# Routed feed-forward: expert results scaled by the token's share and added by indirect DMA onto the output, in place of stored pair rows that are read back

## The reference, cut to what matters

```python
logits = jnp.einsum('bsd,de->bse', input_emb, Wr) + br          # input_emb = layernorm(x); 8 experts
route_w = jax.nn.softmax(logits, axis=-1)
_, topk_idx = jax.lax.top_k(route_w, TOP_K)                     # TOP_K = 2
mask = jax.nn.one_hot(topk_idx, E, dtype=route_w.dtype).sum(-2)
routed = route_w * mask
routed = routed / routed.sum(axis=-1, keepdims=True)            # the two shares of a token
h = jax.nn.relu(jnp.einsum('bsd,edh->ebsh', input_emb, W1) + b1[:, None, None, :])
expert_out = jnp.einsum('ebsh,ehd->ebsd', h, W2) + b2[:, None, None, :]
return jnp.einsum('bse,ebsd->bsd', routed, expert_out)          # and x = x + this is the output
```

## Time and profile before

| What | Value |
|---|---|
| Median of three runs | 2058.24 us (2058.22 to 2061.71) |
| The profiled execution: its own time, its span | 2056.44 us, 2054.1 us |
| Mean granted TensorE clock, share of full speed | 0.956 |
| Start of `routed_ffn` on PE | 1718.7 us |
| First hidden layer, tile 0 | 1770.1 us |
| Hidden layer of tile 2, and of tile 22 | 1790.7 us, 2012.5 us |
| Last matmul ends | about 2028.4 us |
| First and last addition onto X by DVE | 2037.2 us, 2049.9 us |

### The profile page before, as it was taken

The page is one execution under the profiler, slowest core; times in us unless marked ns, Lnnn a source line. Parts: engine busy times, 40 slices in busy tenths (PEclk is TensorE's granted clock), DMA queues, the critical chain, the costliest instruction groups (busy, mean ns, idle before and its releaser), DMA issues. The chain is left out here.

```text
span 2054.1 us, 40735 instructions
## 1 busy us (share of the span) xinstructions
PE 1817.9 (88%) x16084; PEld 1324.4 (64%) x16084; DVE 1519.5 (74%) x3172; ACT 1133.2 (55%) x1916; POOL 158.7 (8%) x129
## 2 busy tenths in 40 slices
PE   7959258997799999999999999988997897799994
PEld 6844155665466666666666666655674466688884
DVE  6987886667777777777777776787766777688886
ACT  3535754556366666666666665526542654467762
POOL 0001300000000000000000000000000100244431
PEclk9979689998999999999999999999999998799997
DMA  6120001003000000000000000010001001577775
GB/s 222 47 79 0 0 1 52 2 3 114 21 22 22 22 21 22 22 22 22 23 24 24 15 1 1 1 53 2 3 21 56 1 3 46 187 255 245 248 258 173
DMA packets 80365, 120.90 MB, mean 59 GB/s; under 512 B 9840, under 2 KB 62512, under 8 KB 80048
## 3 DMA queue, kind: packets, MB, share of 16 engines
q1 hardware_dynamic: 75760, 106.22, 15.6%
q0 software_dynamic: 4416, 12.06, 1.7%
HBM read 103.58 MB, written 14.68 MB: 58 GB/s over the span
## 5 line engine op out<-in xcount | busy, mean ns | idle before, releaser
L2586 PE MATMUL sl_ps_eo<-sl_w,sl_hT 128*128 128x256 f16 x3072 | 353.2, 273 | 0.8 <-DVE sl_hT L2829 0.7
L2563 PE MATMUL sl_ps_h<-sl_slot_inT,sl_w 128*128 128x512 f16 x1536 | 338.3, 379 | 0.5 <-ACT sl_h L2706 0.5
L2586 PEld LDWEIGHTS sl_ps_eo<-sl_w,sl_hT 128*128 128x128 f16 x3072 | 298.5, 98 | 35.8 <-DVE sl_hT L2829 1.3
L2706 ACT ACTIVATE sl_h<-sl_ps_h,sl_b1T 128x512 f32<-128x512 f32 x256 | 175.6, 687 | 170.3 <-PE sl_ps_h L2563 163.3
L2563 PEld LDWEIGHTS sl_ps_h<-sl_slot_inT,sl_w 128*128 128x128 f16 x1536 | 149.9, 98 | 176.3 <-ACT sl_h L2706 2.4
L2829 DVE TENSOR_TENSOR sl_hT<-sl_h,sl_hT 128x512 f16<-128x512 f32 x256 | 176.8, 692 | 102.2 <-ACT sl_hT L2709 97.9
L1149 DVE TENSOR_REDUCE at_neg_max<-at_ps 128x8 bf16<-128x1024 f32 x96 | 116.9, 1220 | 68.2 <-PE at_ps L831 68.2
L2125 PE MATMUL mo_ps_h<-mo_xgT,mo_w 128*128 128x256 f16 x1104 | 125.9, 275 | 3.5 <-issue 2.1
L2843 DVE SCALAR_TENSOR_TENSOR sl_result<-sl_ps_eo,sl_b 128x256 f32<-128x256 f32 x128 | 54.3, 424 | 97.8 <-PE sl_ps_eo L2586 93.5
L2136 PE MATMUL mo_ps_eo<-mo_w,mo_hT 128*128 128x256 f16 x1104 | 124.1, 273 | 0.0
L2125 PEld LDWEIGHTS mo_ps_h<-mo_xgT,mo_w 128*128 128x128 f16 x1104 | 108.1, 99 | 19.0 <-issue 5.8
(11 more groups left out here) (435 smaller groups left out, 3629.8 us busy)
## 6 DMA issues: line engine op xcount, KB each, us to landing
mo_w_raw<-in_L_ffn_W SPq DMA_DIRECT2D x46, 1024.0 KB, 8.7
sl_w_in<-in_L_ffn_w SPq DMA_DIRECT2D x16, 1024.0 KB, 5.4
at_ctxT<-ctx_pairs SPq DMA_DIRECT2D x9, 512.0 KB, 7.3
mo_w_raw<-pair_rows SPq DMA_DIRECT2D x4, 1024.0 KB, 9.0
mo_b<-in_L_ffn_b SPq DMA_DIRECT2D x23, 128.0 KB, 4.9
ac_attention_w<-L_attention_w SPq DMA_DIRECT2D x3, 768.0 KB, 12.4
w_pairs<-ac_w_pair SPq DMA_DIRECT2D x3, 768.0 KB, 3.2
ac_ctx_all<-in_ctx SPq DMA_DIRECT2D x4, 512.0 KB, 8.2
```

What stands on the lines that cost most here:

```text
L2563: last = pe.matmul(ps_h[:, j % 2], w1[:, e % 2, w, k, j * P:(j + 1) * P], slot_inT[:, q % 2, x, k].rearrange("p b s -> p (b s)"), start=(k ...
L2586: last = pe.matmul(ps_eo[:, b % 2, 0:D], hT[:, hp, j, b * P:(b + 1) * P], w2[:, e % 2, w, j], start=(j, a) == (0, 0), stop=(j, a) == (HJ - ...
L2706: act.activation(h[:, j % 2], ps_h[:, j % 2], ACT.Gelu, bias=b1T[:, q // G4, j:j + 1], scale=1.0 / W_SCALE).then_inc(h_ready, 1)
```

## The change

The scaling by the shares moves from the end of the phase into the tile loop, and the sum over a token's two experts moves from DVE to the DMA engines.

- SP writes X to the output at the phase's start (2 MB, and 256 KB more into spare rows behind it); the output tensor has 256 rows more, which the host cuts off.
- A row of `x_rows` grows from 1,024 to 1,032 bytes: behind the two halves stand the token's two shares, written by one DMA in pieces of 8 bytes (2,048 of them) once DVE has them. The gathers wait for it too, and bring the shares with the rows.
- POOL picks the right share of each slot with two small operations (`weigh`), which stand ahead of the tile's gather and scatter.
- ACT multiplies `y` by that share into `y_scaled` (`scaled`), two operations of 128 x 256 a tile, behind the copy of the next tile's rows.
- POOL's scatter adds onto the output (`compute_op=ALU.add`), and waits until the scatters of the tile before have landed, since two experts may add to the same token.
- SP's wait before the biases is now on `result_ready`, DVE's semaphore of `y`; DVE's `y` waits for ACT (`y_ready`) in place of the scatter.
- The read-back, DVE's 32 additions and the final stores are gone; SP only waits for the last scatters.
- DVE makes `to_i` behind `from_i`, and three small operations for the parity of a slot.

```diff
+            sp.dma_start(env.out[0:B * L].rearrange("(b l) d -> l b d", l=L), env.X[:]).then_inc(x_out, 16)
+            sp.dma_start(env.out[B * L:].rearrange("(b l) d -> l b d", l=L), env.X[:, 0:HALVES]).then_inc(x_out, 16)
...
+            sp.wait_ge(share_ready, 1)
+            with nc.allow_non_contiguous_dma("two shares a token"):
+                sp.dma_start(env.x_rows.rearrange("(b l) d -> l b d", l=L)[:, :, D:D + 2], shares[:]).then_inc(shares_out, 16)
             sp.wait_ge(expert_ready, 1)
...
                 if m >= WB:
-                    sp.wait_ge(y_ready, HALVES * (m - WB + 1))
+                    sp.wait_ge(result_ready, HALVES * (m - WB + 1))
...
-            pairs = env.pair_rows[0:2 * B * L].rearrange("(b l i) d -> l b i d", l=L, i=2)
-            for g in range(4):
-                sp.dma_start(yt[:, 4 * g:4 * g + 4], pairs[:, 4 * g:4 * g + 4]).then_inc(y_in[g], 16)
-            for g in range(8):
-                sp.wait_ge(x_done, 2 * (g + 1))
-                sp.dma_start(env.out[2 * g:2 * g + 2].rearrange("b l d -> l b d"), env.X[:, 2 * g:2 * g + 2]).then_inc(stored, 16)
...
+            def scaled(m, s):
+                act.wait_ge(result_ready, HALVES * m + s + 1)
+                act.wait_ge(weight_ready, m + 1)
+                enough(act, scattered[m % 2], 16 * HALVES * (m // 2))
+                act.activation(y_scaled[:, m % 2, s], y[:, m % 2, s], ACT.Copy, scale=weight[:, m % 2, s:s + 1]).then_inc(y_ready, 1)
...
+                if m >= 1:
+                    for s in range(HALVES):
+                        scaled(m - 1, s)
...
+            def weigh(m):
+
+                pool.wait_ge(gathered[m % XB], 16 * HALVES * (m // XB + 1))
+                pool.tensor_tensor(picked[:, m % 2], xg_rows[:, m % XB, :, D:D + 2], of_pair[:, HALVES * m:HALVES * (m + 1)],
+                                   ALU.mult).then_inc(picked_made, 1)
+                pool.wait_ge(picked_made, m + 1)
+                enough(pool, y_ready, HALVES * (m - 1))
+                pool.tensor_tensor(weight[:, m % 2], picked[:, m % 2, :, 0], picked[:, m % 2, :, 1], ALU.add).then_inc(weight_ready, 1)
+
             def scatter(m):
+                if m >= 1:
+                    pool.wait_ge(scattered[(m - 1) % 2], 16 * HALVES * ((m - 1) // 2 + 1))
                 for s in range(HALVES):
                     q = HALVES * m + s
                     pool.wait_ge(y_ready, q + 1)
-                    pool.indirect_dma_start(env.pair_rows, bass.IndirectOffsetOnAxis(ap=to_i[:, q:q + 1].bitcast(U32), axis=0),
-                                            y[:, m % 2, s], None).then_inc(scattered[m % 2], 16)
+                    pool.indirect_dma_start(env.out, bass.IndirectOffsetOnAxis(ap=to_i[:, q:q + 1].bitcast(U32), axis=0),
+                                            y_scaled[:, m % 2, s], None, compute_op=ALU.add).then_inc(scattered[m % 2], 16)
...
                 dve.wait_ge(eo_made, HALVES * m + s + 1)
-                enough(dve, scattered[m % 2], 16 * HALVES * (m // 2))
+                enough(dve, y_ready, HALVES * (m - 1))
```

More of the change, by code:

```diff
@@ L1955, in routed_ffn @@
         ratio = t.sb("ratio", [P, B, 1])
-        share = t.sb("share", [P, 2, B, 1])
+        shares = t.sb("shares", [P, B, 2])
         hit = t.sb("hit", [P, 2, B, E])
@@ L2015, in routed_ffn @@
         h_made, h_ready, h_high, h_split = (t.sem(n) for n in ("h_made", "h_ready", "h_high", "h_split"))
-        eo_made, y_ready = t.sem("eo_made"), t.sem("y_ready")
+        eo_made, result_ready, y_ready = t.sem("eo_made"), t.sem("result_ready"), t.sem("y_ready")
+        share_ready, shares_out = t.sem("share_ready"), t.sem("shares_out")
+        to_ready, of_pair_ready = t.sem("to_ready"), t.sem("of_pair_ready")
+        picked_made, weight_ready = t.sem("picked_made"), t.sem("weight_ready")
+        x_out = t.sem("x_out")
         scattered = [t.sem(f"scattered{i}") for i in range(2)]
-        y_in = [t.sem(f"y_in{i}") for i in range(4)]
-        first_added, x_done, stored = t.sem("first_added"), t.sem("x_done"), t.sem("stored")
         block = ctx.enter_context(nc.Block())
@@ L2197, in _ @@
                     tokens_out(m + 1)
+                if m >= 1:
+                    for s in range(HALVES):
+                        scaled(m - 1, s)
+            for s in range(HALVES):
+                scaled(NTILES - 1, s)
         @block.gpsimd
@@ L2258, in _ @@
             dve.wait_ge(ratio_ready, 1)
-            link(dve.tensor_scalar(share[:, 1], ratio[:], 1.0, None, ALU.add))
-            link(dve.reciprocal(share[:, 0], share[:, 1]))
-            link(dve.tensor_tensor(share[:, 1], share[:, 0], ratio[:], ALU.mult))
+            link(dve.tensor_scalar(shares[:, :, 1:2], ratio[:], 1.0, None, ALU.add))
+            link(dve.reciprocal(shares[:, :, 0:1], shares[:, :, 1:2]))
+            dve.tensor_tensor(shares[:, :, 1:2], shares[:, :, 0:1], ratio[:], ALU.mult).then_inc(share_ready, 1)
             dve.wait_ge(ranked, 1)
@@ L2297, in _ @@
             link(dve.scalar_tensor_tensor(spare[:], used[:], 1.0, spare_row[:], ALU.subtract, ALU.mult))
-            dve.tensor_tensor(to_i[:], pair[:], spare[:], ALU.subtract)
             dve.tensor_scalar(from_i[:], pair_i[:], 1, None, ALU.logical_shift_right).then_inc(table_ready, 1)
+            dve.tensor_scalar(parity_i[:], pair_i[:], 1, None, ALU.bitwise_and).then_inc(of_pair_ready, 1)
+            dve.wait_ge(table_ready, 1)
+            dve.tensor_tensor(to_i[:], from_i[:], spare[:], ALU.subtract).then_inc(to_ready, 1)
             link.done()
+            dve.wait_ge(of_pair_ready, 1)
+            dve.tensor_copy(of_pair[:, :, 1], parity_i[:]).then_inc(of_pair_ready, 1)
+            dve.tensor_scalar(of_pair[:, :, 0], parity_i[:], -1.0, 1.0, ALU.mult, ALU.add).then_inc(of_pair_ready, 1)
             def split_high(m, p):
@@ L2346, in _ @@
                 result(NTILES - 1, s)
[L2348 to L2360, removed]
 def newton_rsqrt(dve, link, out, var, half, tmp):
@@ L3066, in constants @@
                         - B * L).reshape(P, 2 * B),
-        "spare_row": 2 * B * L + np.arange(NQ)[None, :] * P + row[:, None],
+        "spare_row": B * L + np.arange(NQ)[None, :] % HALVES * P + row[:, None],
     }
```

37 lines of the change are left out of this document (23 added, 14 removed).

## The result

The changed kernel takes 2046.32 us (median of six runs, 2043.54 to 2047.92) where the kernel before, timed beside it, takes 2056.49 (2053.88 to 2061.71): a ratio of 0.9943, interval 0.9927 to 0.9959, so 8 to 15 us less. The prediction was 2048.4 us. Its profiled execution has a span of 2045.5 us against 2054.1.

A forecast was written before the change was run, and what follows sets the result against it. Bounds: DVE's additions and waits after the last result, and in the loop a two-tile ring slightly longer than PE. Terms -19.4, +7.4, +2.0 and +0.2 sum to -9.8, off the 2058.24 us median: 2048.4 us, range 2038 to 2064.

The forecast's parts named there:

- the end: After the last y: scaling, POOL's start, scatter landing and barrier take 5.9 us in place of 25.29, so -19.4.
- the ring: Tile loop: W1's landing, ACT, DVE's y, SP's next W1 issue; one round over two tiles takes 22.66 us.
- POOL's start 0.28 later: At the end: POOL starts the last scatter 0.28 us after the scaling, the wait between tiles being covered.
- Scatter-adds in the ring: Tile loop: adds take twice a copy's DMA engine time and delay W1, +7.4 us, between 0 and +22.
- all of it ahead of W1's landing: Tile loop: the adds' whole extra 0.74 us an engine per tile was assumed to delay W1.
- the formula: Tile loop: lengthening the ring by d costs about d/2 a tile, 10 d over 20 tiles.
- the rival of slow adds: Adds at 4.5 copies' engine time make the kernel slower, 2067 us; the sign turns at 1.23 us; chance 0.17.
- the estimate of 6.9 us: Tile loop: the scatter-add term if an add costs 1.93 times a copy, as the skill measured.
- ACT and POOL beside DVE: Tile loop: ACT's scalings remove play and POOL's operations contend with DVE, +2.0 us, between 0 and +4.
- The start: Phase start: writing X and the shares fits before the first gather, +0.2 us, between -0.5 and +2.
- the rival of late shares: Phase start: at 0.2 us a piece the shares land late and delay the first gather, 2058 us; chance 0.08.
- The rival of hidden adds: Tile loop: adds fit into idle DMA time, the loop costs at most 2.0 us, about 2040; chance 0.20.

The follow-up runs named there:

- e8: Changed kernel with POOL's weights and gathers ahead of a tile's adds, and DVE making tile 21's first half result before the last tile's fourth split: 2046.47 us, ratio 0.9931.
- e1: Changed kernel with the addition left out, so scatters overwrite output rows as plain copies: ratio 0.9937 to the kernel before.
- e7: Changed kernel with POOL's next weights and gather ahead of a tile's adds, and ACT's scaling after the next tile's second W1 copy: ratio 0.9969.
- e11: Changed kernel without ACT's scaling and POOL's multiplications, the plain results being added: 2042.81 us, ratio 0.9908.
- e4: Changed kernel without POOL's two multiplications a tile, ACT scaling by a constant column: ratio 0.9936.
- e2: Changed kernel with odd tiles adding onto a region of their own, so adds wait only for the tile before last: ratio 0.9952.
- e10: Changed kernel with POOL waiting at its end until its last adds have landed: ratio 0.9936.
- e9: Changed kernel with each tile's second half added once more, onto a region nobody reads: 2059.38 us, ratio 0.9995.
- e5: Changed kernel run again unchanged, to show the spread of single profiles: 2047.24 us, ratio 0.9938.

## Why the prediction was right, and where it was not

The total came out within 2.1 us of the forecast (the change is -10.2 us by the medians, -9.8 by the sum). For the larger part, the end, the mechanism was the named one. That the sum agrees is luck: the end was put 5.9 us too good and the ring 7.4 too bad, and the two errors nearly cancel. None of the three signs that were to show it right came: the span ends 11.7 us after the last `y` and not some 6, the tile stretch takes 225.0 us and not 230 to 232, and a lone add has 3.4 times a scatter's DMA time and not twice.

- **The end: -19.4 predicted, -13.5 measured** (25.3 to 11.8, two profiles each). Scaling 0.5 and barrier 1.2 were about right (0.55 and 1.0). So was the landing: 2.43 plus 1.5 for the add was 3.9, and it took 3.7. Two steps failed. "POOL's start 0.28 later" became 2.58, because the wait for tile 21 was not covered and the two halves are issued one after the other at 1.57 us, not 1.0: 2.3 us. The landing that the wait needed was near the 3.9 that the prediction allowed; but it put tile 21's second issue 4.0 us ahead of the last `y` (2028.39 less 2023.85 and 0.5), and it came only 2.4 ahead (2031.03 against 2033.42). And POOL's drain was not in the sum, since in the old profile DVE's additions covered it: 3.8 us. Together these are 6.1; less 0.3 by which landing and barrier were shorter, they are the 5.8 by which 11.66 exceeds the 5.9 of the sum. e8 shows the first of them: bringing tile 21's adds forward takes 1.3 to 1.7 us off the tail.
- **Scatter-adds in the ring: +7.4 predicted, nothing seen.** The failed step is "all of it ahead of W1's landing". The price was too low, if anything: in the loop an add keeps each engine busy for 0.9 us (a copy's 0.37 and e1's difference of 0.53), and by the formula that would be +10.6. A lone add takes 0.42 of 5.92 us for two, 1.24 each, past the 1.23 at which the rival of slow adds was to turn the sign. Yet W1's landing stays where it was: 10.0 and 10.2 us in the median of the old kernel's two profiles and 10.2 in e1, all without adds, 10.0 with two a tile, 10.3 with three. So the busy share of the add's queue is not time taken from the loads' queue. Whether the engines work on other packets meanwhile no row shows.

```profile
2035.08:2041.00 5.92, 0.00 (x0) 0.00 (x0) 0.00 (x0) 0.00 (x0) 3.15 (x2) 0.71 0.42 44
```

- The Trainium skill (Collectives: The Full Stack, section "The bandwidth ceiling: the fold count and why AG ≠ RS ≠ AR") has a reduction between cores at 1.93 times a copy. The traces here have 2.4 times in the loop and 3.4 alone, in busy time; in the loop's length they show no difference, and the estimate of 6.9 us worked out from that ratio failed with mine.
- **ACT and POOL beside DVE: +2.0 predicted, the whole loop lost 2.0.** The number agrees, the cause is not shown. ACT's new least distance from `y` to `w1_out` is there as worked out (1.98), but e7 and e11 remove it and the loop stays at 225; e4 removes POOL's operations and stays in the spread. Nor does DVE work longer beside POOL: it is busy for 188.94 us of the loop before and 188.10 after. Each of the four suspects alone (the addition, the wait for the tile before, ACT's scaling, POOL's weighing) is worth less than the 2 us that a profile can tell; that they make the loss together is not excluded. What else is left is in all these runs: rows of 1,032 bytes, and scatters onto the output. Neither was tried apart. In tile 22 the scaling may cost 0.3 to 0.8 us, which the sum did not have.
- **The start: +0.2 predicted, nothing told from the spread.** The 2,048 pieces of 8 bytes landed 4.1 us after their issue, far inside the bound of 13.6, and the first gather is issued 39.1 us after the phase's first matmul (40.7 before), so the rival of late shares falls. The rule on less than 512 bytes (the Trainium skill, DMA: Bandwidth & Descriptors, section "Specifications") would speak of a price here; no run shows one that matters.

```profile
x_rows<-mo_shares SPq DMA_DIRECT2D x1, 16.0 KB, 4.1
```

The rival of hidden adds described the loop best; it gave 2040 only because it kept the quick end. Of the markers that I named, "POOL waiting for its own scatters in every tile" was a bad one: it came true in 14 of 20 tiles and cost nothing that shows (e2).

## What to carry to other kernels

When a change takes away the work at the end of a program, list every engine's own closing wait before summing: one that lay behind the removed work becomes the end. The busy share of a DMA queue is no price by itself; look whether another queue's landing moves when it is doubled. And before a step that an in-order queue waits for is moved, write down what stands behind it there: scaling some 4 us later on ACT cost 50 us through POOL's gathers, and a few lines of POOL's order gave them back.

## What the runs showed of the hardware

- POOL's drain after an indirect DMA: it ended 3.8 us after SP had seen the last add land (nine profiles, to within 0.01; 5.9 to 6.1 after the end of that add's issue), 6.1 after a copy's landing (e1), 4.6 after its own start where POOL had waited for the landing (e10, 4.8 after the landing), and 0.9 after the landing in e9. What it waits for stays open.
- POOL issues an add onto DRAM in 1.57 us alone and 1.76 in the loop, a copy of the same rows in 0.97 and 1.04.
- A lone add lands 3.7 us after its issue, a lone copy after 2.4; in the loop 9.0, with a copy's 7.4 in e1 and 4.7 in the kernel before.
- Equal code gives tile loops of 222.8 to 225.0 us (changed, e5, e10). The ring turns a few late landings of W1 (10.8 to 12.1 us for a median of 10.0 in the changed kernel and e5) into stalls, and it doesn't make them up: no tile takes less than 10.92.
